# Attention with a fused 1x1 convolution: chunk 7's keys and queries handed to other engines, and the first subtraction taken in two parts

## What is computed

```python
q = einsum('oc,bcn->bon', Wq, xf) + bq      # 32 channels
k = einsum('oc,bcn->bon', Wk, xf) + bk      # 32 channels
v = einsum('oc,bcn->bon', Wv, xf) + bv      # 256 channels
att = softmax(einsum('bdi,bdj->bij', q, k) / sqrt(32), axis=-1)
out = gamma * einsum('bcj,bij->bci', v, att)
fused = einsum('oc,bcn->bon', Wf, concat([out, xf])) + bf
```

## Time and profile before

| | |
|---|---|
| median of 3 runs | 1962.97 us |
| the profiled execution | 1963.01 us |
| its span | 1961.2 us |
| TensorE matmul busy | 99% |
| ScalarE busy | 87% |
| VectorE busy | 86% |
| GpSimd busy | 72% |
| granted TensorE clock, mean | 0.998 |

### The profile page before, as it was taken

The page is one execution under the profiler, slowest core; times in us unless marked ns, Lnnn a source line. Parts: engine busy times, 40 slices in busy tenths (PEclk is TensorE's granted clock), DMA queues, the critical chain, the costliest instruction groups (busy, mean ns, idle before and its releaser), DMA issues.

```text
span 1961.2 us, 46458 instructions
## 1 busy us (share of the span) xinstructions
PE 1942.1 (99%) x15656; PEld 1912.5 (98%) x15656; DVE 1683.6 (86%) x2700; ACT 1710.9 (87%) x2282; POOL 1413.3 (72%) x689
## 2 busy tenths in 40 slices
PE   9999999999999999999999999999999999999998
PEld 8899999999989999999998999999999999999998
DVE  7888989887888889888688888889868898888996
ACT  7899999997789999999788999999978899999996
POOL 3778777778477787777747777877765777777775
PEclk9999999999999999999999999999999999999999
DMA  4311111110321111111032111111104111111111
GB/s 144 84 22 18 16 22 22 21 18 16 125 73 23 20 17 17 22 21 22 12 132 65 23 22 18 17 18 21 22 12 136 38 23 22 21 18 17 19 22 17
DMA packets 297816, 69.70 MB, mean 36 GB/s; under 512 B 280528, under 2 KB 281296, under 8 KB 297680
## 3 DMA queue, kind: packets, MB, share of 16 engines
q1 hardware_dynamic: 296864, 67.90, 15.9%
q10 hardware_dynamic: 816, 0.13, 0.0%
HBM read 34.41 MB, written 33.55 MB: 35 GB/s over the span
## 4 chain that ended last, share of the span: by engine, by line
PE 94%; DVE 2%; POOL 1%; issue 1%; ACT 1%; DMA 0%; SPq 0%; DVEq 0%; ACTq 0%; POOLq 0%
PE ps_o L429 74%; PE ps_s L421 11%; PE ps_o L293 3%; PE ps_p L293 3%; PE ps_s L310 1%; DVE top L675 1%; PE ps_p L328 1%; PE ps_p L324 1%; ACT raw L514 0%; POOL kq_rest L921 0%; DMA raw<-wf1T 0%; DVE top_j L680 0%; POOL queries L924 0%; DVE lo L721 0%; DVE raw L716 0%
## 5 line engine op out<-in xcount | busy, mean ns | idle before, releaser
L875 POOL TENSOR_TENSOR raw<-raw,top_m 128x1024 f32<-128x1024 f32 x508 | 1208.6, 2412 | 259.8 <-DVE top_m L710 241.9
L429 PE MATMUL ps_o<-val_hi,hi 128*128 128x258 f32 x4096 | 1003.9, 283 | 7.2 <-DVE val_lo L789 7.2
L429 PE MATMUL ps_o<-val_lo,hi 128*128 128x256 f32 x4096 | 1001.6, 281 | 0.0
L429 PEld LDWEIGHTS ps_o<-val_hi,hi 128*128 128x128 f32 x4096 | 775.4, 190 | 8.5 <-DVE val_lo L789 5.7
L429 PEld LDWEIGHTS ps_o<-val_lo,hi 128*128 128x128 f32 x4096 | 772.9, 189 | 0.0
L721 DVE TENSOR_TENSOR lo<-ps_p,hi 128x1024 fp32r<-128x1024 f32 x512 | 622.5, 1216 | 153.7 <-ACT ps_p L602 147.8
L675 DVE TENSOR_TENSOR top<-ps_s,top 128x512 f32<-128x512 f32 x960 | 658.5, 686 | 65.9 <-ACT raw L514 12.2
L595 ACT ACTIVATE hi<-raw 128x1024 fp32r<-128x1024 f32 x508 | 539.4, 1062 | 146.1 <-PE ps_o L429 133.9
L429 PE MATMUL ps_o<-val_hi,lo 128*128 128x258 f32 x4096 | 600.3, 284 | 0.7 <-DVE lo L721 0.6
L514 ACT ACTIVATE raw<-ps_s 128x512 f32<-128x512 f32 x1024 | 553.3, 592 | 30.6 <-DVE top L675 5.4
L429 PEld LDWEIGHTS ps_o<-val_hi,lo 128*128 128x128 f32 x4096 | 537.6, 190 | 1.8 <-DVE lo L721 1.3
(11 more groups left out here) (76 smaller groups left out, 1103.9 us busy)
## 6 DMA issues: line engine op xcount, KB each, us to landing
xf<-x SPq DMA_DIRECT2D x32, 512.0 KB, 3.7
conv_d<-conv_st SPq DMA_DIRECT2D x64, 256.0 KB, 2.0
result<-conv_d SPq DMA_DIRECT2D x512, 32.0 KB, 1.8
out<-result SPq DMA_DIRECT2D x510, 32.0 KB, 1.6
raw<-wf2T SPq DMA_DIRECT2D x1, 256.0 KB, 5.0
raw<-wv SPq DMA_DIRECT2D x1, 256.0 KB, 4.2
raw<-wf1T SPq DMA_DIRECT2D x1, 256.0 KB, 5.4
raw<-wkqT ACTq DMA_DIRECT2D x1, 64.0 KB, 2.5
```

The lines of the kernel that those rows point to most:

```text
L429: last = nc.tensor.matmul(ps_o[:, i, 0:width], p[:, t % 2, jl * I + i * P:jl * I + (i + 1) * P], v[:, j, 0:width], start=opens and jl == 0 ...
L875: nc.gpsimd.tensor_tensor(raw[:, slot], raw[:, slot], top_m[:, r].unsqueeze(1).broadcast_to((P, JQ, I)), ALU.subtract).then_inc(sub_done, 1)
```

## The change

Five things change.

1. Chunk 7's keys: ScalarE writes the second band too, from the first (semaphore `k_doubled`), and then goes on to the scores of chunk 6; the raw queries (`q_keep`) follow after these. GpSimd's copy of these keys is gone.
2. The low part of chunk 7's queries is made by VectorE (`last_queries`, two instructions) in quad 0 of block 0, between the splitting of quad 0 and that of quad 1, and no longer by GpSimd in chunk 7. TensorE waits for it in quad 7 of block 0 and not in quad 2.
3. `subtract_first` is called for each half by itself, and the two `values_lo` stand between the halves.
4. Chunk 0 of the first image is loaded by two DMAs, and rounded and split in halves, with semaphores of their own.
5. `wvf_split` is signalled after the weights, the bias has its own semaphore, and `setup_values` comes ahead of the queries' low part in chunk 0.

```diff
@@ sync
-            load_x(0, 0)
+            for k in range(KT):
+                sp.dma_start(xf[:, 0, k], x_v[0:1, :, k, 0:W].rearrange("b p n -> p (b n)")).then_inc(x0_loaded[k], 16)
+            sp.sem_inc(x_loaded[0], 16)
@@ tensor
-                    pe.wait_ge(x_hi_done, C + 1)
                     for k in range(KT):
+                        if first and c == 0 and k == 0:
+                            pe.wait_ge(x0_hi_half, 1)
+                        else:
+                            pe.wait_ge(x_hi_done, C + 1)
...
                 if last_chunk:
                     pe.wait_ge(k_out, C + 1)
-                    pe.wait_ge(k_copied, C + 1)
+                    pe.wait_ge(k_doubled, b + 1)
...
-                    if first and t == 2:
+                    if first and t == QUADS - 1:
 
                         pe.wait_ge(q_out, b * CHUNKS + CHUNKS)
                         pe.wait_ge(q_copied, b * CHUNKS + CHUNKS)
@@ scalar
+            def split_first():
+
+                for k in range(KT):
+                    act.wait_ge(x0_loaded[k], 16)
+                    nc.scalar.activation(hi[:, 0, k * W:(k + 1) * W], xf[:, 0, k], ACT.Copy).then_inc(
+                        x0_hi_half if k == 0 else x_hi_done, 1)
...
+                    if c == CHUNKS - 1:
+
+                        act.wait_ge(k_hi_done, C + 1)
+                        nc.scalar.activation(keys[CK:2 * CK, span(c)], keys[0:CK, span(c)].bitcast(F32),
+                                             ACT.Copy).then_inc(k_doubled, 1)
+                        return
...
+                def q_keep(c, C):
+                    act.wait_ge(q_out, C)
+                    nc.scalar.activation(q_raw[2 * CK:P], ps_p[2 * CK:P, 0], ACT.Identity,
+                                         bias=bkkqq[2 * CK:P]).then_inc(q_raw_done, 1)
...
                     kq_hi(c + 1, C + 1)
                     early_scores(c)
+                    q_keep(c + 1, C + 1)
@@ vector
-                                               ALU.mult, ALU.subtract)
-                nc.vector.scalar_tensor_tensor(bias[:], ps_s[:, 0, 0:KT, 0], gam, bf_c, ALU.mult, ALU.add).then_inc(wvf_split, 1)
+                                               ALU.mult, ALU.subtract).then_inc(wvf_split, 1)
+                nc.vector.scalar_tensor_tensor(bias[:], ps_s[:, 0, 0:KT, 0], gam, bf_c, ALU.mult,
+                                               ALU.add).then_inc(bias_done, 1)
...
                     spread_top(b * BLOCKS, 0)
-                    subtract_first(b * BLOCKS)
+                    subtract_first(b * BLOCKS, 0)
                     values_lo(0)
                     values_lo(1)
+                    subtract_first(b * BLOCKS, 1)
                     split_p(b * STEPS, 0)
...
+            def last_queries(C):
+
+                at = span(CHUNKS - 1)
+                dve.wait_ge(q_copied, C)
+                nc.vector.tensor_tensor(kq_rest[R3:P], q_raw[2 * CK:R3], queries[2 * CK:R3, at].bitcast(F32),
+                                        ALU.subtract).then_inc(q_rest_done, 1)
+                dve.wait_ge(q_rest_done, C)
+                nc.vector.tensor_tensor(queries[CK:2 * CK, at], q_raw[R3:P], kq_rest[R3:P], ALU.add).then_inc(q_out, 1)
...
+                    if t == 0 and first:
+                        last_queries(b * CHUNKS + CHUNKS)
@@ gpsimd
-                pool.wait_ge(k_hi_done, C + 1)
-                pool.sem_inc(kq_seen, 1)
-                nc.gpsimd.tensor_copy(keys[CK:2 * CK, span(c)], keys[0:CK, span(c)]).then_inc(k_copied, 1)
+                if c < CHUNKS - 1:
+                    pool.wait_ge(k_hi_done, C + 1)
+                    pool.sem_inc(kq_seen, 1)
+                    nc.gpsimd.tensor_copy(keys[CK:2 * CK, span(c)], keys[0:CK, span(c)]).then_inc(k_copied, 1)
+                else:
+
+                    pool.sem_inc(k_copied, 1)
...
+                    if c < CHUNKS - 1:
+                        pool.wait_ge(q_copied, C + 1)
+                        pool.wait_ge(q_out, C)
+                        nc.gpsimd.tensor_tensor(kq_rest[R3:P], q_raw[2 * CK:R3], queries[2 * CK:R3, span(c)].bitcast(F32),
+                                                ALU.subtract).then_inc(q_rest_done, 1)
+                        pool.wait_ge(q_rest_done, C + 1)
+                        nc.gpsimd.tensor_tensor(queries[CK:2 * CK, span(c)], q_raw[R3:P], kq_rest[R3:P],
+                                                ALU.add).then_inc(q_out, 1)
+                if c == CHUNKS - 1:
                     pool.wait_ge(q_copied, C + 1)
...
-                if c == CHUNKS - 1:
-                    pool.wait_ge(q_out, C + 1)
                     pool.wait_ge(sub0_done, b + 1)
```

More of the change, by code:

```diff
@@ L123, in attention_conv @@
         wkq_split, wf2_split, wvf_split = sem("wkq_split"), sem("wf2_split"), sem("wvf_split")
+        bias_done = sem("bias_done")
         wvf_ready, id_zeroed, id_made, ones_done = sem("wvf_ready"), sem("id_zeroed"), sem("id_made"), sem("ones_done")
+        x0_loaded = [sem(f"x0_loaded{k}") for k in range(KT)]
+        x0_hi_half, x0_split = sem("x0_hi_half"), sem("x0_split")
         x_loaded = [sem(f"x_loaded{i}") for i in range(2)]
@@ L531, in kq_hi @@
                     else:
-                        act.wait_ge(q_out, C)
-                        nc.scalar.activation(q_raw[2 * CK:P], ps_p[2 * CK:P, 0], ACT.Identity,
-                                             bias=bkkqq[2 * CK:P]).then_inc(q_raw_done, 1)
+                        q_keep(c, C)
+                def q_keep(c, C):
+                    act.wait_ge(q_out, C)
+                    nc.scalar.activation(q_raw[2 * CK:P], ps_p[2 * CK:P, 0], ACT.Identity,
+                                         bias=bkkqq[2 * CK:P]).then_inc(q_raw_done, 1)
                 def conv_out(src, ot, C=C):
@@ L566, in project @@
                 if start:
-                    split_x(0, 0)
+                    split_first()
                     act.wait_ge(wf2_loaded, 16)
@@ L662, in split_x, with split_first @@
                                         ALU.subtract).then_inc(x_split, 1)
+            def split_first():
+                for k in range(KT):
+                    dve.wait_ge(x0_hi_half if k == 0 else x_hi_done, 1)
+                    nc.vector.tensor_tensor(lo[:, 0, k * W:(k + 1) * W], xf[:, 0, k], hi[:, 0, k * W:(k + 1) * W].bitcast(F32),
+                                            ALU.subtract).then_inc(x0_split if k == 0 else x_split, 1)
             def fold_scores(base, made, old, new, halves=(0, 1), at_once=False):
@@ L710, in spread_top, with subtract_first @@
                 nc.vector.transpose(top_m[:, r], top_all[:].unsqueeze(2).broadcast_to((P, I // 32, 32))).then_inc(m_done, 1)
-            def subtract_first(B):
+            def subtract_first(B, half):
                 dve.wait_ge(m_done, B + 1)
[L714 to L717, removed]
+                two = raw[:, 0, 2 * half:2 * half + 2]
+                nc.vector.tensor_tensor(two, two, top_m[:, 0].unsqueeze(1).broadcast_to((P, 2, I)),
+                                        ALU.subtract).then_inc(sub0_done if half else sub0_half, 1)
             def split_p(Q, t):
@@ L766, in kq_lo, with k_lo @@
                 def kq_lo(c, C):
+                    k_lo(c, C)
+                    q_lo(c, C)
+                def k_lo(c, C):
                     dve.wait_ge(k_hi_done, C + 1)
@@ L773, in kq_lo, with q_lo @@
                                             ALU.add).then_inc(k_out, 1)
+                def q_lo(c, C):
                     if c >= LATE:
@@ L813, in project @@
                     finish_image(b)
-                kq_lo(c, C)
+                k_lo(c, C)
+                if start:
+                    setup_values()
+                q_lo(c, C)
                 if c == CHUNKS - 2:
                     split_x(C + 1, c + 1)
-                if start:
-                    setup_values()
                 values_lo(0)
@@ L918, in project @@
                     nc.gpsimd.tensor_copy(queries[0:CK, span(c)], queries[2 * CK:R3, span(c)]).then_inc(q_copied, 1)
-                    pool.wait_ge(q_copied, C + 1)
-                    pool.wait_ge(q_out, C)
-                    nc.gpsimd.tensor_tensor(kq_rest[R3:P], q_raw[2 * CK:R3], queries[2 * CK:R3, span(c)].bitcast(F32),
-                                            ALU.subtract).then_inc(q_rest_done, 1)
-                    pool.wait_ge(q_rest_done, C + 1)
-                    nc.gpsimd.tensor_tensor(queries[CK:2 * CK, span(c)], q_raw[R3:P], kq_rest[R3:P],
-                                            ALU.add).then_inc(q_out, 1)
-                if c == CHUNKS - 1:
-                    pool.wait_ge(q_out, C + 1)
+                    if c < CHUNKS - 1:
[7 more added lines that the diff above has]
+                if c == CHUNKS - 1:
+                    pool.wait_ge(q_copied, C + 1)
                     pool.wait_ge(sub0_done, b + 1)
```

8 lines of the change are left out of this document (6 added, 2 removed).

## The result

| | before | after |
|---|---|---|
| median | 1963.13 us (1962.93 to 1963.24, 6 runs) | 1977.63 us (1975.49 to 1980.01, 6 runs) |
| ratio after / before | | 1.0074, 95% interval 1.0063 to 1.0084 |
| profiled execution, span | 1963.01 us, 1961.2 us | 1978.32 us, 1976.5 us |
| mean granted TensorE clock | 0.998 | 0.995 |

The change makes the kernel 14.5 us slower. The forecast was 1972.1 us, with a range up to 1977: the sign held and so did the lost turns, but the measured time lies 0.6 us above the range, because the price of TensorE's clock behind the new stall was put far too low. The page's busy line answers to the earlier trace rows: hardly any work was added, so the loss is waiting and a slower clock.

The account below looks back on a forecast made before the run. TensorE, with matmuls in flight 1942.1 us of a 1961.2 us span, was taken to bound the kernel. Profiled 1963.01 + 8.0 (four images at +2.0) + 1.1 (clock) - 0.0 (start) = 1972.1 us; range 1961.5 to 1977.

Parts of the forecast that it names:

- the lost turns: Main case, chance 0.57: VectorE's two new low-query instructions each wait behind a GpSimd subtraction; `lo` products 3.2 us late.
- the price of TensorE's clock behind the new stall: Clock at 0.50 after TensorE's new 3 us idle stretch: 0 to 4.4 us in four images, 1.1 taken.
- parts 1 and 2 of the prediction: Chunk 7: folding starts 0.77 us earlier, and L680 loses 0.58 us once GpSimd's low-query instruction is gone.
- S: Moment VectorE reaches the first subtraction of block 0 in an image; forecast to come 1.35 us earlier.
- part 3 of the prediction: First subtraction in halves, block 0: `sub0_done` 1.21 us later against S, at S+2.50; quad 1 starts at S+6.50.
- the rival that let it start earlier with the freed banks: Quad 1 not held by GpSimd's first subtraction starts 1.35 us earlier per image: 1957.6 us, chance 0.07.
- part 4 of the prediction: Low queries on VectorE before quad 1, block 0: two turns lost, `lo` products at S+12.08, +2.0 us an image net.
- the rival of one lost turn: Second new VectorE instruction slips in ahead of waiting GpSimd: +0.3 us an image, 1964.2 us, chance 0.16.
- the rivals without a turn lost: Contention does not touch the two 32-row VectorE instructions, which fit in 2.05 us idle time: 1962 us, chance 0.13.
- with GpSimd keeping its turn: First new VectorE instruction waits out GpSimd's back-to-back subtractions, until S+19.25: near 2008 us, chance 0.07.
- The step from S+12.08 to the reference point: From quad 1's `lo` products to the chain's 32-matmul piece ending block 0: 22.64 us, plus 0.1; point at S+34.8.
- part 5 of the prediction: Kernel start, waiting for `wf1`: halves and second DMA give nothing, the bias 0.14 us; together 0.0 to -0.14.

Follow-up runs that it names:

- The third: The changed kernel with chunk 7's low queries back on GpSimd and the first subtraction's halves next to each other again: 1960.22 us, ratio 0.9985.
- first experiments: The changed kernel with chunk 7's low queries back on GpSimd, all else as changed: 1964.62 us, ratio 1.0009.
- The second: The changed kernel with GpSimd's second subtraction in block 0 waiting until VectorE's two new low-query instructions are done: 1972.10 us, ratio 1.0045.
- seventh: The kernel before plus two VectorE instructions of 32x508, both inputs from SBUF, results unused, ahead of quad 1 of block 0: 1975.55 us, ratio 1.0068.
- eighth experiments: The kernel before plus two VectorE transposes of 32x512, one SBUF input each, ahead of quad 1 of block 0: 1962.94 us, ratio 0.9999.
- sixth experiment: The changed kernel plus 24 TensorE matmuls with zeros ahead of the wait for `lo` in quad 1 of block 0: 1971.67 us, ratio 1.0042.
- fifth experiment: The changed kernel with only the first subtraction's two halves put next to each other again: 1976.85 us, ratio 1.0062.
- fourth experiment: The kernel before with only chunk 0 in halves and the bias signalled by itself: 1962.69 us, ratio 0.9997.

## Why the prediction was right in direction, and short in size

**Keys and scores (parts 1 and 2 of the prediction, up to S): right.** S came 1.19 us earlier in the first image and at 559.66 in the second, of which 3.59 us are the lateness inherited from the first image: 557.37 + 3.59 - 559.66 = 1.30 earlier; in the third and fourth, worked out in the same way, 1.31 and 1.20. Forecast was 1.35. L716 takes 0.42 in chunk 7, and the folds follow without a pause:

```profile
553.50 3.08 DVE L711 TENSOR_TENSOR top<-ps_s,top 128x512 f32<-128x512 f32 x4
556.62 0.42 DVE L716 TENSOR_TENSOR top_j<-top 128x256 f32<-128x256 f32 x1
```

**The halves (part 3 of the prediction): right.** `sub0_done` is at 71.43 + 0.68 = S+2.49, forecast S+2.50, and it carries GpSimd, which starts 0.17 us behind it at 72.28. TensorE's quad 1 starts at 76.07, S+6.45, forecast S+6.50, so the rival that let it start earlier with the freed banks is out. The third and first experiments give 4.4 us for the halves alone, where 1.21 an image makes 4.8.

**The low queries (part 4 of the prediction): the mechanism and its size right.** Both instructions wait for a subtraction of GpSimd and end about 0.55 behind it; the second never went ahead of GpSimd, in any image, so the rival of one lost turn is false, and so are the rivals without a turn lost (2.75 us for 0.69 of work) and with GpSimd keeping its turn (17.34 us for seven subtractions, and the pair done after the second and third). The products with `lo` came at S+12.02 to S+12.06 for S+12.08. The second, seventh and eighth experiments show the cause apart from all else: it goes when GpSimd is quiet, comes into the kernel before with such a pair, and stays away with one SBUF input. The Trainium skill's page "SBUF — State Buffer", section "Who interferes with whom", is borne out by these three. That the first issuer keeps the port for its whole instruction is said there of VectorE's two-port modes; the 2.74 us here show it for this form as well. The 115 ns of the Trainium skill's section "A bandwidth-pool intuition that's wrong" on the same page were measured on DMA descriptors that GpSimd writes beside a VectorE copy; here they opened no gap for an instruction issued 0.03 us behind.

**The step from S+12.08 to the reference point: wrong, by the clock.** This is the term that failed: 1.1 us once for the granted clock, where the runs show 6 to 7 us. The sum took 22.64 + 0.1 us an image for it, and 1.1 us once for the clock. Measured are 24.22, 23.97, 24.26 and 25.38 us, which is 7.3 us over four times 22.64, where the forecast had 4 x 0.1 + 1.1 = 1.5. The difference, 5.8 us, is about what is missing between 1972.1 and the 1977.63 measured. The sixth experiment shows what it is: with TensorE busy through the stall, all else being the same, the clock stays at 1.00, the points return to S+34.8 in three images, and 5.96 us come back between the medians. The two profiled executions give nearly the same: 1978.32 - 1973.90 = 4.4 us, and the 2.3 us of the third turn that only the second of them lost make 6.7. The distances of the reference points in the changed kernel (36.24, 36.03, 36.30 and 37.42 less 34.8 each) add up to 6.8. The fifth experiment shows it once more, without any added matmul: where the clock stayed at 1.00 behind the same stall, the step was 22.74.

The prediction had both numbers in hand: "A new idle stretch of 3 us lies on the path, so 0 to 4.4 us in four images; I take 1.1, since part of it will lie within waits." Two things were wrong with that. The drop came in four images of four, not in one. And its price was read from the second image of before, where 3 to 4 us of low clock moved the start of quad 1 by 1.1 us and the reference point by less (0.4 us against the third image, whose clock stayed at 1.00). Behind the new stall TensorE waits for nobody up to the reference point, and ScalarE waits for TensorE, so every slow matmul counted: 1.2 to 1.5 us in three images, and 2.6 in the fourth, where the clock was low for twice as long. The upper end of the range carried the same price and fell short with it. Nor does the drop come behind every such stall: the fifth experiment has an image without it.

**The start (part 5 of the prediction): right.** The first product of values starts at 12.80 us, before at 12.81: `wf1` landed 0.12 later, the bias was 0.14 less. The fourth experiment finds nothing beyond that which is clear of the noise.

## What to carry to other kernels

Before moving a small VectorE instruction with two SBUF inputs, look at what GpSimd does at the new place: here, with GpSimd running without a pause, each such instruction waited for one whole GpSimd instruction, two that depend on each other for two, and whatever stood behind them on VectorE paid; with one input from SBUF it was free. When a sum puts a new TensorE stall of about 3 us on the path, let the upper end of the range have the clock at half speed for some microseconds behind it in every repetition, at 1.2 to 2.6 us each as here, and do not take the price from a row where the slow stretch lay elsewhere. And take parts of a change one by one: of these five, the keys and the start together gained 2.9 us, and the other two gave back 17.4.

## What the runs showed of the hardware that was not expected

Stalls of TensorE of 2.6 to 3.1 us in quad 1 were followed by a granted clock of 0.50 in four images of four of the changed kernel, for 3 to 7 us; 24 matmuls with zeros in that stall kept the clock at 1.00 and made the kernel 6 us faster. It is not certain, though: in the fifth experiment the clock stayed at 1.00 behind a stall of 3.05 us and fell behind those of 2.88, 4.12 and 4.51, and in the seventh it fell behind one of four stalls of 1.76 to 2.13 us. What decides it was not measured.

VectorE idled 1.75 to 2.04 us before the first new instruction in the second and third image, with nothing in the profile that it waited for, and not in the first and fourth. This is so in all six kernels with two instructions at that place: the changed one and those of the second, fifth, sixth, seventh and eighth experiments, the transposes included. What sets these two images apart was not isolated, so the cause stays open. It is free where the instruction must wait anyway, and costs a third turn where it makes it miss a subtraction by 0.06 us. Not tried: the low queries at another place, where GpSimd pauses.
